# A two-layer image block on one core: three bands of replicas, the low halves on GpSimd, a new instruction order, per-head weights

## The reference

```python
# layer 0, with _gn a group norm over 32 groups of 4 channels
xn  = x / norm_over_channels(x) * g * C ** 0.5
q, k, v = split(einsum('bchw,oc->bohw', xn, w_qkv), 3)        # 4 heads of 32
k, v = concat([mem_k, k]), concat([mem_v, v])                  # 4 memory columns
q = softmax(q, over channels of a head) * scale;  k = softmax(k, over pixels)
context = einsum('bhdn,bhen->bhde', k, v)
out = einsum('bhde,bhdn->bhen', context, q)
x = x + einsum('bchw,oc->bohw', out, w_out) + b_out
# layer 1
w3m = w3 * ((j - i) % 4 == 0);  w1m = w1 * ((j - i) % 4 != 0)
x = x + conv3x3(_gn(x), w3m) + einsum('oi,bihw->bohw', w1m, _gn(x)) + b1.sum(1)
```

## Time and profile before

| | us |
|---|---|
| median of 3 runs | 2020.36 (2018.03 to 2023.75) |
| the profiled execution, its own time | 2011.88 |
| its span | 2010.1 |
| PE busy in the span | 1882.8 (94%) |
| DVE busy | 1676.3 (83%) |
| ACT busy | 1361.0 (68%) |
| POOL busy | 1321.8 (66%) |
| replicas, high halves: DMAs, KB, us to landing | 256 of 165.0 KB, 3.6; 256 of 107.2 KB, 2.3 |
| replicas, low halves | 128 of 165.0 KB, 4.1; 128 of 107.2 KB, 2.3 |

### The profile page before, as it was taken

One profiled execution on the slowest core, in us unless ns is written; L12 is line 12 of the kernel. 1 busy time (PEld: TensorE's weight loads), 2 busy tenths in 40 slices (PEclk: granted clock), 3 DMA queues, 4 the chain that ended last, 5 costly groups with the idle time before them and its releaser, 6 DMA issues.

```text
span 2010.1 us, 50737 instructions
## 1 busy us (share of the span) xinstructions
PE 1882.8 (94%) x21199; PEld 1017.6 (51%) x21199; DVE 1676.3 (83%) x3144; ACT 1361.0 (68%) x1476; POOL 1321.8 (66%) x737
## 2 busy tenths in 40 slices
PE   2889999999999999999999999999999999999995
PEld 0445545555544555554555554455554455555452
DVE  5688888888888888888888888888888888888862
ACT  2667668767667776766876766777766777676660
POOL 5566667776667676666776665777666767666652
PEclk9789999999999999999999999999999999999997
DMA  5358778787877797876878777778787778787665
GB/s 108 64 96 176 162 159 162 160 177 160 165 162 160 156 183 154 174 163 159 161 161 170 165 163 156 154 167 177 152 175 154 162 155 180 148 174 162 130 132 129
DMA packets 349427, 312.96 MB, mean 156 GB/s; under 512 B 299152, under 2 KB 299920, under 8 KB 341008
## 3 DMA queue, kind: packets, MB, share of 16 engines
q1 hardware_dynamic: 347712, 308.73, 73.8%
q10 hardware_dynamic: 1168, 0.98, 0.2%
q0 software_dynamic: 320, 0.01, 0.0%
HBM read 68.10 MB, written 67.11 MB: 67 GB/s over the span
## 4 chain that ended last, share of the span: by engine, by line
PE 66%; DVE 17%; SPq 9%; DMA 4%; issue 2%; ACT 1%; POOL 0%; ACTq 0%
PE pair_ps L813 21%; PE pair_ps L795 8%; PE pair_ps L756 6%; PE pair_ps L804 4%; PE bank_ps L710 4%; DVE u L1121 4%; DVE km L1124 3%; PE pair_ps L776 3%; SPq L320 2%; DVE yg_lo L1171 2%; SPq L333 2%; DVE image L1176 2%; DVE bn L1045 2%; PE bank_ps L786 2%; PE pair_ps L741 2%; PE bank_ps L765 2%
## 5 line engine op out<-in xcount | busy, mean ns | idle before, releaser
L813 PE MATMUL pair_ps<-replicas,w_rep 96*32 96x512 f16 x8192 | 490.5, 384 | 11.7 <-DMA replicas<-yg_lo 11.3
L441 POOL TENSOR_TENSOR u_lo<-u,u_hi 128x1024 f16<-128x1024 f32 x128 | 270.3, 2144 | 274.3 <-ACT u_hi L558 274.3
L444 POOL TENSOR_TENSOR exp_kT_lo<-exp_kT,exp_kT_hi 128x1024 f16<-128x1024 f32 x128 | 273.6, 2137 | 206.4 <-ACT exp_kT_hi L567 203.4
L813 PEld LDWEIGHTS pair_ps<-replicas,w_rep 96*32 96x32 f16 x8192 | 204.4, 96 | 260.1 <-issue 85.2
L447 POOL TENSOR_TENSOR u_lo<-exp_q,u_hi 128x1024 f16<-128x1024 f32 x128 | 272.6, 2141 | 45.5 <-ACT u_hi L573 44.7
L558 ACT ACTIVATE u_hi<-u 128x1024 f16<-128x1024 f32 x128 | 134.9, 1054 | 134.8 <-DVE u L1121 130.1
L1176 DVE SCALAR_TENSOR_TENSOR image<-pair_ps,image 128x512 f32<-128x512 f32 x256 | 176.0, 688 | 55.0 <-PE pair_ps L813 49.4
L437 POOL TENSOR_SCALAR u<-image,st 128x1024 f32<-128x1024 f32 x128 | 179.6, 1411 | 40.4 <-DVE st L1075 40.4
L564 ACT ACTIVATE exp_kT<-pair_ps,zcol 128x1024 f32<-128x1024 f32 x128 | 142.0, 1109 | 90.3 <-PE pair_ps L756 87.7
L573 ACT ACTIVATE u_hi<-exp_q 128x1024 f16<-128x1024 f32 x128 | 133.9, 1046 | 97.1 <-DVE exp_q L1163 97.1
L454 POOL TENSOR_TENSOR yg_lo<-u,yg_hi 128x1024 f16<-128x1024 f32 x64 | 152.9, 2390 | 68.5 <-ACT yg_hi L581 68.5
(11 more groups left out here) (179 smaller groups left out, 4601.2 us busy)
## 6 DMA issues: line engine op xcount, KB each, us to landing
image<-in_x SPq DMA_DIRECT2D x256, 256.0 KB, 4.8
out<-image SPq DMA_DIRECT2D x512, 128.0 KB, 2.3
replicas<-yg_hi SPq DMA_DIRECT2D x256, 165.0 KB, 3.6
replicas<-yg_hi SPq DMA_DIRECT2D x256, 107.2 KB, 2.3
replicas<-yg_lo SPq DMA_DIRECT2D x128, 165.0 KB, 4.1
replicas<-yg_lo SPq DMA_DIRECT2D x128, 107.2 KB, 2.3
uT_hi<-u_hi SPq DMA_TRANSPOSE x128, 4.4
uT_lo<-u_lo SPq DMA_TRANSPOSE x128, 4.2
```

The lines of the kernel that those rows point to most:

```text
L441: pool.tensor_tensor(px(UL, v), px(U, v), px(UH, v), ALU.subtract).then_inc(ul_ready, 1)
L444: pool.tensor_tensor(KL[:, v % 2], KT[:, v % 2], KH[:, v % 2], ALU.subtract).then_inc(kl_ready, 1)
L813: mm = pe.matmul(conv_ps[32 * r:32 * r + 32, j % 2], w_rep[0:32 * SLOTS, tap, r], rep[:, j * ROWS + dy:(j + 1) * ROWS + dy, dx:dx + SIDE], ...
```

## The change

On the four queues that matter most it does the following.

- The replicas come in three bands of 26, 16 and 24 rows instead of two of 26 and 40; each step then issues 36 replica DMAs instead of 24. In the two later bands the low halves are issued ahead of the high ones.
- All four `low_y` of a sample are on GpSimd.
- The loop's seam is elsewhere: `max_k`, the first two `max_q` and the shift row of a sample are now made in the same stage as its `normalise`. PE's, DVE's, ACT's, POOL's and SP's orders are written anew.
- The mixing matrix: `value_out` and `memory_out` hold, per head, the product of value (or memory) weights and output weights, made once. Per sample there are eight fp32 matmuls with 32 output rows instead of three products with 128 (L832, L833, L836), the mask is gone, and the division by the sums moves into `split_mix`.
- The set-up: sample 1 is loaded only once sample 0 has landed; two memsets go from GpSimd to VectorE; ScalarE permutes the weights; VectorE finishes sample 0's statistics before it waits for any weight; the high and low halves of the convolution's weights are made in the first sample's `high_u` and `rows_q`; the rest of the set-up is in its `norm_power`, `norm_sums` and `norm_guard`.
- The end: the last sample's convolution is a list of its own (`drain`). VectorE makes the group norm and the low halves of y there, and ScalarE's queue issues half of the replicas, the stores of sample 30 and half of the last store.

```diff
-EARLY = 3
-SPLIT = EARLY * ROWS + 2
+BANDS = ((0, 3 * ROWS + 2), (3 * ROWS + 2, 5 * ROWS + 2), (5 * ROWS + 2, PAD))
...
-            for k in range(PRELOADED):
-                load(k, 0)
-                load(k, 1)
+            load(0, 0)
+            load(0, 1)
+            for h in range(2):
+                sp.wait_ge(x_in[h][0], at_load(0))
+            load(1, 0)
+            load(1, 1)
...
                 if c is not None:
                     sp.wait_ge(hi_ready, at(c, UNITS, 2))
                     replicate_high(c, 0)
-                    sp.wait_ge(lo_even, at(c, UNITS // 2, 1))
-                    sp.wait_ge(lo_odd, at(c, UNITS // 2, 1))
+                    sp.wait_ge(lo_ready, at(c, UNITS, 2))
                     replicate_low(c, 0)
-                    sp.wait_ge(hi_ready, at(c, UNITS, 4))
+                    sp.wait_ge(lo_ready, at(c, UNITS, 3))
+                    replicate_low(c, 1)
                     replicate_high(c, 1)
-                    sp.wait_ge(lo_odd, at(c, UNITS // 2, 2))
-                    sp.wait_ge(lo_even, at(c, UNITS // 2, 2))
-                    replicate_low(c, 1)
...
+                    sp.wait_ge(lo_ready, at(c, UNITS, 4))
+                    replicate_low(c, 2)
+                    replicate_high(c, 2)
...
+            def fold_values():
+
+                pe.wait_ge(setup_dve, HEADS_READY)
+                heads = wo_heads.rearrange("p h o -> p (h o)")
+                pe.matmul(pair_ps[0][:, 0:BANK], perm_qkv[:, 2].rearrange("p r i -> p (r i)"), heads, start=True, stop=True)
+                pe.wait_ge(col_in, 16 * COL_DMAS)
+                pe.matmul(pair_ps[0][0:MEM, BANK:2 * BANK], mv[:], heads, start=True, stop=True).then_inc(setup_pe, 1)
...
-            def value_context(ps):
-                pe.matmul(ps[:, 0:P], wqkvT[:, 2], AT_sb[:], start=True, stop=False)
-                pe.matmul(ps[:, 0:P], mvT[0:MEM], pkT_sb[0:MEM], start=False, stop=True).then_inc(mix_pe, 1)
             def mix_weights(ps):
-                pe.matmul(ps[:, 0:P], ctxT_sb[:], woT[:], start=True, stop=True).then_inc(mix_pe, 1)
+
+                for h in range(HEADS):
+                    q = slice(DH * h, DH * h + DH)
+                    pe.matmul(ps[q, 0:P], AT_sb[:, q], value_out[:, h], start=True, stop=False)
+                for h in range(HEADS):
+                    q = slice(DH * h, DH * h + DH)
+                    mm = pe.matmul(ps[q, 0:P], pkT_sb[:, q], memory_out[:, h], start=False, stop=True)
+                mm.then_inc(mix_pe, 1)
...
+            def split_conv_weights():
+                dve.wait_ge(setup_act, TAPS_ROUNDED)
+                make(dve.tensor_tensor(mid32[:, 0], taps32[:, CENTRE], quad_mask[:], ALU.mult))
+                make(dve.tensor_tensor(mid32[:, 1], taps32[:, TAPS], other_mask[:], ALU.mult), wait=True)
+                make(dve.tensor_tensor(mid32[:, 1], mid32[:, 1], mid32[:, 0], ALU.add), wait=True)
+                make(dve.tensor_copy(w_mid[:, 0], mid32[:, 1]), wait=True)
+                dve.tensor_tensor(w_mid[:, 1], mid32[:, 1], w_mid[:, 0], ALU.subtract)
+                make(dve.tensor_tensor(w_lo, taps32[:, 0:TAPS], w_hi, ALU.subtract))
...
+                did = chain(mix_dve, s, 7, 0)
+                did(dve.tensor_tensor(z[:, 0:1], ps[:, P:P + 1], pk_sum[:], ALU.add), wait=False)
+                did(dve.tensor_copy(A_sb[:], ps[:, 0:P]))
+                did(dve.reciprocal(z[:, 1:2], z[:, 0:1]), wait=False)
...
-            def low_y(s, v):
-                dve.tensor_tensor(inner(LO, v), rows(px(YG, v)), inner(HI, v), ALU.subtract).then_inc(lo_even, 1)
...
+            def drain(c, e):
...
+                group_norm_y(c, 0)
+                dve.wait_ge(yg_ready, at(c, UNITS, 1))
+                dve.wait_ge(hi_ready, at(c, UNITS, 1))
+                last_low_y(c, 0)
```

More of the change, by code:

```diff
@@ L281, in image, with over_samples, band @@
             return B[buffer_of(sample)]
[L283 removed]
+        def over_samples(step, drain, after_second=None):
             def known(s):
                 return s if 0 <= s < batch else None
[L288 removed]
+            for s in range(batch + 1):
                 step(known(s), known(s - 1), known(s - 2), known(s - 3))
[L290 to L291 removed]
+                if s == 1 and after_second is not None:
+                    after_second()
+            drain(batch - 1, batch - 2)
+        def band(half):
+            first_row, end_row = BANDS[half]
+            return slice(first_row * PAD, end_row * PAD)
         block = ctx.enter_context(nc.Block())
@@ L393, in _ @@
+            over_samples(step, drain, replicate_weights)
             for v in range(UNITS):
@@ L712, in norm_sums @@
                 mm.then_inc(norm_sum, 1)
+                if first(s) and v == UNITS - 1:
+                    fold_values()
             def broadcast(ps, v, done):
```

791 lines of the change are left out of this document (467 added, 324 removed).

## The result

The changed kernel takes 2051.3 (2050.0 to 2052.8, 4 runs) against 2022.1 (2018.0 to 2026.9, 4 runs) of the kernel before: a ratio of 1.0147, with a 95% interval of 1.0131 to 1.0163. It is slower by 1.5%, and outside my range of 1960 to 2014. Its profiled execution has a span of 2049.3 against 2010.1, at a granted clock of 0.984 against 0.983.

A forecast was written before the change was run, and what follows sets the result against it. A steady step was TensorE's work (57.3) plus VectorE's longer stretch (2.0): 59.3. Savings of 10 (start), 3 (steps 1 and 2), 9 (29 steps) and 7 (end), 29, plus 1 for late loads, took 2020.36 to 1990; range 1960 to 2014.

The forecast's parts named there:

- The start: Set-up to first keys: sample 0's statistics no longer wait for weights; first keys at 50.7, 10 less (bounds 6 and 12).
- the end: Last sample's drain: VectorE makes group norm and low halves, queues share DMAs and last store; 7 less (4 to 9).
- TensorE's work: Steady step: 1.15 a sample leaves, eight small mixing matmuls add about 0.45; net 0.7 less, 57.3 a step.
- Low halves on GpSimd: Steady step: two low halves move from VectorE to GpSimd, then 45 busy of 59; covered, neither engine binding there.
- Outside the stretch TensorE should hardly wait: Steady step outside first `residual` to shift row: next image's group means and the transpose are covered by other work.
- VectorE's 2.0 in the stretch: From first `residual` to shift row, VectorE takes 20.6 against TensorE's 18.6, adding 2.0 a step.
- Rival 1: Steady step: VectorE's stretch doesn't bind and TensorE runs at 57.8 a step; 1948, chance 0.17.
- rival 2: Steady step: chunk 3 waits for replicas of band 1, 2.5 a step; 2064, chance 0.09.
- Steps 1 and 2: First steps: weights' split partly hidden, shorter mixing chain gives 2 to 3; together 3 less (0 to 5).
- Rival 4: Start and first steps: set-up work moved behind sample 0 holds them; 4 won instead of 13, 1999; no separate chance.
- Rival 3: Ends gain and steady steps lose the same, 60.2 to 60.5 a step; 2015 to 2026, no change, chance 0.09.
- Three bands: Replica DMAs: twelve more cost SyncE's queue 7.6 a step, but chunk 3's low half stays hidden by 0.2, narrowly.

The follow-up runs named there:

- experiment 1: Changed kernel, but GpSimd waits for VectorE's last `den_parts` before the low half of y of unit 3: 2030.5, ratio 1.0073.
- experiment 5: Changed kernel with GpSimd waiting for `den_parts`, `norm_sums` 0 and 1 side by side, and the weights' split behind sample 1's statistics: 2000.3, ratio 0.9899.
- experiment 6: The kernel of experiment 5, with the denominators moved behind the context of unit 2, as in the kernel before: 1990.9, ratio 0.9852.
- experiment 8: The kernel of experiment 6, with `turn_k_max` issued ahead of the last rough product of q: 1989.4, ratio 0.9858.
- experiment 9: The kernel of experiment 6, with unit 0's rough product and `max_q` behind the shift row, unit 1's behind the next `keys` 0: 1994.8, ratio 0.9886.
- experiment 4: Changed kernel, but `split_conv_weights` stands behind sample 1's statistics and scale, not ahead of them: 2049.0, ratio 1.0162.
- experiment 7: The kernel before with three bands of replicas, later bands' low halves first, nothing else changed: 2018.3, ratio 0.9986.

## Why the prediction was wrong

The step that failed is the sum of the steady step, 57.3 of work and 2.0 of standing still. The work was 58.9, as what moves did not keep its price, and 0.5 of new waits came from VectorE's instructions that GpSimd holds up. By the prediction's own terms, in us a steady step (busy and still from the stretches):

| | TensorE busy | still | step |
|---|---|---|---|
| forecast | 57.3 | 2.0 | 59.3 |
| before | 58.0 | 1.6 | 59.61 |
| after | 58.9 | 2.3 | 61.23 |
| 1: GpSimd waits | 58.7 | 1.7 | 60.49 |
| 5: and `norm_sums`, weights | 57.9 | 1.8 | 59.66 |
| 6: and denominators | 57.6 | 1.8 | 59.37 |

- **The start** (10 less) and **the end** (7 less) came as worked out: 10.2 and 6.6. One sign was a slip: the last sample's taps were to start 33 ahead of the end of the span, but 1980.63 is 29.5 ahead of it, and 3.5 earlier in an end that is 7 shorter makes 26; measured, it is 25.7, and a gap of 5.21 is left in front of it, where 6.82 was.
- **TensorE's work** failed: "Net 0.7 less: 57.3 a step". It is 1.6 more. I priced what is added and taken away (the new mixing product takes 0.57 where I had 0.45), and took everything that moves at its old price. But small matmuls are cheap only beside their like: the eight records of `norm_sums` of two units take 1.06 together, and the four of one unit 1.03. The busy time of `norm_sums`, the denominators and the broadcasts in the steady stretch, in the changed kernel:

```profile
178.71:1954.47 1775.76, 90.59 (x464) 18.39 (x464) 1.00 0.75 158
178.71:1954.47 1775.76, 67.49 (x464) 15.51 (x464) 1.00 0.75 158
178.71:1954.47 1775.76, 78.91 (x464) 19.23 (x464) 1.00 0.75 158
```

  and in the kernel before:

```profile
179.86:1908.69 1728.83, 81.35 (x464) 15.57 (x464) 1.00 0.78 163
179.86:1908.69 1728.83, 55.79 (x464) 12.10 (x464) 1.00 0.78 163
179.86:1908.69 1728.83, 67.85 (x464) 16.69 (x464) 1.00 0.78 163
```

  That is 0.3, 0.4 and 0.4 more a step for the same matmuls. The order listings ahead of the prediction showed the broadcasts taken apart (x2 in place of x4), the new order had `norm_sums` 0 and 1 apart, and the earlier trace rows had the 1.06 of four side by side. The 0.3 is itself a balance: units 0 and 1 cost 1.0 more, and units 2 and 3, which took 1.74 before since unit 3's squares came 0.7 late, take 1.04 and give 0.7 back, which was not in my sum either. Experiments 5 and 6 gave the loss of `norm_sums` 0 and 1 and that of the denominators back. The remaining 0.4 of the 1.6 lies in small amounts over the other groups (counted from start to start, the centre taps have 0.2 of it), and no experiment looked at it.
- **"Low halves on GpSimd"** failed: "neither of the two engines binds at that place". I added GpSimd's list up only for when it ends, and was right on that (ahead of the low halves of q it still waits for ScalarE, 141.8 in all). What it does to others while it runs I left out, and the sign stood in the earlier trace rows: the low halves on VectorE at 1218, 1492 and 3896 ns (min, median, max), those on GpSimd at up to 3063. One instruction of one shape that takes three times its minimum is being held by something. I used the 3063 as a bound for lateness, and asked no further. The ratio of the two speeds, on which I saw the trace agree with about two, is 1.4 to 1.8 by these rows; the loss did not come from it.
- **"Outside the stretch TensorE should hardly wait"** failed with it: 0.66 a step at the broadcast and the centre taps, of which 0.5 is gone in experiment 1.
- **VectorE's 2.0 in the stretch** was right: in the late step of the changed kernel the stretch takes 20.5 (1627.95 to 1648.48; forecast 20.6), TensorE stands still for 1.7 to 1.8 a step in the kernels of this order whose `den_parts` are free (0.6, 0.5, 0.3 and small ones), and that VectorE closes it fits experiments 8 and 9. Rival 1 is out, and so is rival 2.
- **Steps 1 and 2** (3 less) were 9.0 more. The split of the weights, which I had as "partly hidden", stood ahead of the statistics that everybody waits for; it costs 4.5 in step 1 (experiment 4). Step 2 stays long; its granted clock is 0.93 against 0.95, and why it rises later than before wasn't tried. Rival 4 had this effect in view for the first steps (4 won in place of 13 with the start; it was 1.1), but as a case inside my range.
- **Rival 3** (the steps lose, 60.2 to 60.5, as slow small instructions stand in a loop closed over VectorE; chance 0.09) had the direction and a part of the mechanism; the step was 61.2, beyond it. Slower by more than 6 had a chance of 0.10.
- **Three bands** were hidden, as forecast (experiment 7).

With a wait on GpSimd, `norm_sums` 0, the denominators and the split of the weights put back, the change gives 1990.9 and a step of 59.37, where the forecast was 1990 and 59.3. The step comes near with both of its terms, 57.6 and 1.8, though gains and losses that I had not counted balance in the first. That the time comes out is luck in part. Of the profiled execution, from which the sum started, the forecast was 1983 and this version's took 1992.2: steps 1 and 2 are together 3.5 longer than before where I had 3 less. What about closes the difference is the 8.5 by which the profiled execution of the kernel before lies under its median, which I carried over and which this version does not have.

## What to carry to other kernels

Before moving elementwise work to GpSimd, list the VectorE instructions with all operands in SBUF that will run beside it, and see whether one of them is on the chain; a wait on the engine that has time can be a gain. Price what is moved as well as what is added: on TensorE, matmuls with 32 output rows went side by side here only while they stood next to each other and their inputs were ready together. In a hand-ordered loop, follow the cycle once around, engine by engine, and charge each edit to both parts.
